# A two-layer cross-attention network on one Trainium2 core: three positions moved in the self-attention's hand-written order

## The reference

```
x1 = x  + MHA(LN(x), LN(ctx))          # layer 0 cross-attention, 16 heads of 32
x2 = x1 + MLP(LN(x1))                  # layer 0, hidden width 2048
x3 = x2 + MHA(LN(x2), LN(x2))          # layer 1 self-attention  <- the change is in here
x4 = x3 + MHA(LN(x3), ctx)             # layer 1 cross-attention
x5 = x4 + MLP(LN(x4))                  # layer 1, hidden width 2048
```

## Time and profile before

| | |
|---|---|
| median of three runs | 3421.28 us |
| the profiled execution | 3420.01 us |
| its span, first to last instruction | 3418.2 us |
| mean granted TensorE clock over the span | 0.962 of 2.4 GHz |
| the self-attention stage | from about 1280 to 2257 us of the span |
| idle of TensorE in it for the low part of the attention output (L105) | 26.7 us in 8 waits, the longest 10.3 |

### The profile page before, as it was taken

How to read it: one execution, slowest core, us unless ns; L and a number is a source line. 1 busy time by engine, 2 the same in 40 slices (tenths; PEclk the granted TensorE clock), 3 DMA queues, 4 the chain that set the end, 5 groups by cost and what they waited for, 6 DMA issues and landing times. The chain is left out here.

```text
span 3418.2 us, 41927 instructions
## 1 busy us (share of the span) xinstructions
PE 3165.7 (93%) x14480; PEld 2513.7 (74%) x14480; DVE 1801.5 (53%) x2848; ACT 1573.0 (46%) x2980; POOL 1322.0 (39%) x1355
## 2 busy tenths in 40 slices
PE   6599997999999977999999999849999799999999
PEld 5378776888888855777777777537878588888887
DVE  4588863322322224777777777748887432222221
ACT  2366653322222214766676677626666332222222
POOL 0344441333333332666666666734554111111110
PEclk8799998999999987999999999979999899999999
DMA  4423213211111114443344334331321321111000
GB/s 139 120 58 84 86 53 120 77 50 50 50 44 50 38 48 120 110 119 100 105 123 121 107 105 109 93 105 52 90 81 56 111 81 37 38 37 38 29 30 29
DMA packets 215045, 264.33 MB, mean 77 GB/s; under 512 B 78459, under 2 KB 100579, under 8 KB 214835
## 3 DMA queue, kind: packets, MB, share of 16 engines
q1 hardware_dynamic: 214835, 261.66, 25.7%
HBM read 125.12 MB, written 60.42 MB: 54 GB/s over the span
## 5 line engine op out<-in xcount | busy, mean ns | idle before, releaser
L1101 DVE TENSOR_REDUCE L1sa_nmax<-L1sa_s 128x2 f32<-128x1024 f32 x256 | 310.6, 1213 | 159.9 <-PE L1sa_s L907 159.9
L1206 POOL TENSOR_TENSOR L1sa_El<-L1sa_E,L1sa_Eh 128x1024 fp32r<-128x1024 f32 x128 | 313.3, 2448 | 150.6 <-ACT L1sa_Eh L1000 142.7
L468 DVE TENSOR_TENSOR L1ff_gl<-L1ff_gf,L1ff_gh 128x512 fp32r<-128x512 f32 x128 | 94.9, 741 | 475.0 <-ACT L1ff_gh L428 475.0
L468 DVE TENSOR_TENSOR L0ff_gl<-L0ff_gf,L0ff_gh 128x512 fp32r<-128x512 f32 x128 | 97.1, 759 | 439.8 <-ACT L0ff_gh L428 439.8
L414 ACT ACTIVATE L1ff_gf<-L1ff_f,cols 128x512 f32<-128x512 f32 x128 | 88.3, 690 | 450.8 <-PE L1ff_f L94 450.8
L414 ACT ACTIVATE L0ff_gf<-L0ff_f,cols 128x512 f32<-128x512 f32 x128 | 88.3, 690 | 450.4 <-PE L0ff_f L94 450.4
L1009 ACT ACTIVATE L1sa_E<-L1sa_st 128x1024 f32<-128x1024 f32 x256 | 258.6, 1010 | 8.8 <-PE L1sa_st L919 8.7
L92 PE MATMUL L1ff_f<-L1ff_hTh,L1ff_Wh 128*128 128x512 f32 x512 | 203.3, 397 | 5.7 <-POOL L1ff_hTl L235 5.7
L92 PE MATMUL L0ff_f<-L0ff_hTh,L0ff_Wh 128*128 128x512 f32 x512 | 203.1, 397 | 5.7 <-POOL L0ff_hTl L235 5.7
L1000 ACT ACTIVATE L1sa_Eh<-L1sa_E 128x1024 fp32r<-128x1024 f32 x192 | 200.5, 1044 | 0.2
L94 PE MATMUL L1ff_f<-L1ff_hTl,L1ff_Wh 128*128 128x512 f32 x512 | 200.4, 391 | 0.0
(11 more groups left out here) (282 smaller groups left out, 8514.4 us busy)
## 6 DMA issues: line engine op xcount, KB each, us to landing
L1sa_OLN<-L1sa_osb SPq DMA_DIRECT2D x128, 192.0 KB, 2.6
L0ff_xs<-x SPq DMA_DIRECT2D x64, 256.0 KB, 2.9
L1sa_stack_q<-L1sa_parts_q SPq DMA_DIRECT2D x128, 128.0 KB, 2.6
L1sa_stack_k<-L1sa_parts_k SPq DMA_DIRECT2D x128, 128.0 KB, 2.6
L1ff_xs<-x SPq DMA_DIRECT2D x64, 256.0 KB, 3.3
L0ca_xs<-in_x SPq DMA_DIRECT2D x32, 256.0 KB, 3.0
L0ca_stage<-in_x SPq DMA_DIRECT2D x32, 256.0 KB, 2.8
x<-L0ca_stage SPq DMA_DIRECT2D x32, 256.0 KB, 2.0
```

Source lines behind the costliest of these rows:

```text
L468: nc.vector.tensor_tensor(gl[:, j % 2, :], gf[:, j % 2, :], f32(gh[:, j % 2, :]), ALU.subtract)\
L1101: nc.vector.reduce_max(nmax[:, h % 2, 2 * (n % 2):2 * (n % 2) + 2], s_bank[:, :, :], AX.X, negate=True)\
L1206: nc.gpsimd.tensor_tensor(El[:, n % 2, :], E[:, n % 3, :], f32(Eh[:, n % 2, :]), ALU.subtract)\
```

## The change

Three positions in the written order change, and two DMA positions with them; no instruction is added or removed, and no buffer changes.

- T1, the transposition of the second tile of h, moves from half 24 to half 26 of the block, on TensorE, and with it the two instructions that take its result: ACT's and DVE's from s = 12 to s = 13.
- On SP the load of tile 3 of the next block's h moves from s = 13 to s = 14, and the load of tile 1 of the block after that from s = 16 to s = 17.
- `o_hi` on ACT and `o_lo` on DVE move: for group 0 of a block from n = 8g + 16 to 8g + 17 (s = 17), for the groups 1, 2 and 3 from n = 8g + 12 to 8g + 11 (s = 19, s = 27, and s = 3 of the next block).

```diff
-SA_T_HALVES = (22, 24, 28, 30)
+SA_T_HALVES = (22, 26, 28, 30)
...
-                    if s in (12, 13) and b + 1 < B:
-                        load(b + 1, 2 + (12, 13).index(s))
-                    if s in (15, 16) and b + 2 < B:
-                        load(b + 2, (15, 16).index(s))
+                    if s in (12, 14) and b + 1 < B:
+                        load(b + 1, 2 + (s - 12) // 2)
+                    if s in (15, 17) and b + 2 < B:
+                        load(b + 2, (s - 15) // 2)
...
-                        if n == 8 * g + (16 if g % G == 0 else 12):
+                        if n == 8 * g + (17 if g % G == 0 else 11):
                             o_hi(g)
...
-                        if n == 8 * g + (16 if g % G == 0 else 12):
+                        if n == 8 * g + (17 if g % G == 0 else 11):
                             o_lo(g)
```

## The result

The changed kernel takes 3467.38 us (median of four runs, 3462.45 to 3471.11) where the one before takes 3423.08 us beside it: the ratio is 1.0129, with a 95% interval of 1.0111 to 1.0147. It is slower, as forecast, but by 44 us and not by 22: the time lies 5 us above the upper end of the range. The profiled execution took 3465.93 us, its span is 3464.1 us, and the mean granted clock is 0.959.

A forecast was written before the change was run, and what follows sets the result against it. TensorE, busy 93% of the span, was taken as the bound. O0 - 23.2, ACT + 11.5, T3 + 27.8, clock + 13 and recovery - 5.5 gave + 23.6 on 3420.01 us: forecast 3443, range 3420 to 3462 us.

The forecast's parts named there:

- is done before O0 is due: At s = 3, the moved `o_lo` stands behind the earlier scores' maximum and finishes before TensorE's O0 needs it.
- its 0.7 us: At s = 19, group 0's `o_lo` delays DVE's `o_inverse` by 0.7 us; ACT's 0.5 us waits become 1.1.
- O0: TensorE at s = 4: seven waits for `o_lo` go, gaining 17.7 us plus 5.5 of clock, 23.2 us.
- Group 0: Its `o_hi` and `o_lo` moving from s = 16 to s = 17 was costed at nothing.
- ACT's term: ACT's `o_hi` meets POOL's `onorm`, so `exp` is late: 0.5 us at 23 places, 11.5 us lost, between 0 and 25.
- What is late next: nothing, rather the reverse.: At s = 16 to 18, SP, POOL and DVE catch up while TensorE waits: 5.5 us back, between 0 and 7.
- T3: Tile 3's transposition waits for its late load: 3.76 us in six blocks, 5.2 in block 0, 27.8 us, plus 13 of clock.
- The three waits without a fall: Three of seven O0 waits in the kernel before cost no clock, so the clock loss needn't come every time.
- The sum: Against 3420.01 us: - 23.2 + 11.5 + 27.8 + 13 - 5.5 = + 23.6, so 3443.6 us.
- The third rival: ACT's late `exp` costs 1.1 us at 23 places, clock 2.5 us in seven blocks: + 47, 3467 us; chance 0.07.
- The range's lower end: The forecast's own range, from its clock and ACT bounds, was 3425 to 3462 us.

The follow-up runs named there:

- experiment 8: Kernel before, with TensorE waiting for group 3's `o_lo` only at O0's fourth quarter and at the first for group 2's: 3397.03 us, ratio 0.9930.
- experiment 5: Kernel before, with tile 3's load at s = 14 and group 0's `o_hi` and `o_lo` at s = 17, other groups unmoved: 3469.77 us, ratio 1.0143.
- experiment 6: Kernel of experiment 5, with POOL's `e_lo` in step 17 cut to 16 of its 1024 columns: 3449.56 us, ratio 1.0086.
- experiment 2: Kernel before, with only `o_hi` and `o_lo` moved as in the change: 3425.90 us, ratio 1.0011.
- experiment 3: Changed kernel, with tile 3's load first in s = 14, ahead of `line_up` and the eight copies: 3424.23 us, ratio 1.0007.

## Why the prediction was wrong

**The step that failed** is the cost of the moved `o_lo`. I took its duration from its old places (0.68 to 0.98 us) to its new ones: "is done before O0 is due", "its 0.7 us" at s = 19, and group 0, which "I cost at nothing". All its old places are in even steps, where DVE has its own `e_lo`, and POOL has nothing beside it or shorter instructions (but for one place in the last block, where it meets the end of an `e_lo`); all its new ones are in odd steps, where POOL has its `e_lo`, and there `o_lo` ends half a us after POOL's instruction. I looked at who waits for whom, never at who runs beside whom. The trace of before had the sign: the earlier trace rows show group 3's `o_lo` at 0.98 us where groups 0 and 2 take 0.68, and I passed over it. What stands beside it there is POOL's rounding of the probabilities:

```profile
1578.52 1.04 POOL L1199 CAST L1sa_Eh<-L1sa_E 128x1024 fp32r<-128x1024 f32 x1
```

It ends at 1579.56, and `o_lo` at 1579.12 + 0.98 = 1580.10, 0.54 us later: about the distance that the 28 long ones have in the changed kernel.

**O0: - 23.2 forecast, - 14.8 measured.** The wait of 2.3 us became one of 0.9, because `o_lo` takes 2.58 us; step 4 takes 4.6 us in the seven blocks where 3.39 was forecast. The clock no longer falls behind any of the seven (granted clock 1.00 in the 4 us behind each), so that part of the term came. The sum was right in size for a wait that really goes (experiment 8: - 23.5). That POOL's `e_lo` makes the 0.9 us is worked out from the trace; no experiment shortened POOL's instruction at step 3.

**Group 0: nothing forecast, some 18 to 22 us measured**, and not in its own step but two steps on, as a wait for the row maximum. This is the largest error. Experiments 5 and 6 show it: moving group 0 in the presence of T3's wait costs 22 us, and shortening POOL's instruction beside it gives 20 back. The prediction did see that group 0's `o_lo` pushes `o_inverse` back, as a bound of ACT's term, but at 0.7 us and with ACT as the one that waits for it.

**"What is late next: nothing, rather the reverse."** The recovery was real: steps 17 and 18 gave back 7.2 us, where 5.5 was forecast. But that recovery brings POOL on time, and so its `e_lo` lies on `o_lo`. Without T3's wait (experiments 2 and 3) POOL is late, and group 0's `o_lo` gets ahead of `e_lo`. So the term that I booked as a gain set up the loss. Nothing in the sum could hold this, since it is in neither part alone.

**T3: 27.8 + 13 forecast, 38.8 measured** in steps 15 and 16. The wait is 3.6 to 3.8 us in blocks 1 to 6, against 3.76 forecast; block 0 has 4.5 where 5.2 was forecast, and its T2 waits 1.4 us instead of 0.6. Beyond the waits steps 15 and 16 lost another 1.6 to 2.5 us in each of the seven blocks, 13.0 together, which I put down to the clock: it fell during or behind all seven waits, to a mean of 0.50 to 0.74 in the 3 us behind. The three waits without a fall, on which the prediction's doubt rested, were waits of 2.3 us. This step, the decisive one for the sign, was right in place and size.

**ACT's lateness: + 11.5 forecast;** L919's waits for ACT rose by 11.4 us, in 20 more places instead of 23.

**The sum:** O0 fell short by 8.4 us, and steps 19 and 20 have 22.1 us where ACT's 4 was forecast: 26.5 us, against a miss of 22.3 on the profiled execution; the rest are small differences the other way. The third rival has the right total, 3467 us, by luck: ACT's part came out at its forecast, and it had no collision on DVE in it. The range's lower end was mis-added as well: by the prediction's own bounds it is 3420.0 - 23.2 + 27.8 - 5.5 = 3419, not 3425, which doesn't bear on the miss.

## What to carry to other kernels

Moving an instruction on its engine's order also moves it beside other instructions of other engines: before its duration is carried over, look at what POOL does in the new place, above all if the moved one is on DVE and reads two SBUF tiles. When a change adds a wait, follow who catches up during it, since an engine that is suddenly on time can collide where it was late before. And a wait can often be removed at the reader, by waiting only at the part that reads the late data: here that brought the time to 0.9930 of the kernel before (0.9916 to 0.9945), where `o_hi` and `o_lo` a step earlier gave nothing (1.0011) and `o_lo` ahead of the maximum gave less (0.9953).

## What the runs showed of the hardware

DVE's subtraction of two SBUF tiles of 128x512 takes 0.68 us alone; issued beside a POOL subtraction of 2.4 us it took 2.28 to 2.59 us in 28 of 32 cases of the changed kernel, and in all 28 it ended some 0.55 us after POOL's. Beside a POOL cast of 1.04 us it took 0.98. The other way round POOL's instruction takes longer: in the changed kernel's last block `o_lo` is issued 0.04 us ahead of `e_lo`, keeps its 0.68 us, and `e_lo` takes 2.88 instead of 2.4:

```profile
2238.28 0.68 DVE L105 TENSOR_TENSOR L1sa_oTl<-L1sa_onorm,L1sa_oTh 128x512 fp32r<-128x512 f32 x1
...
2238.32 2.88 POOL L1206 TENSOR_TENSOR L1sa_El<-L1sa_E,L1sa_Eh 128x1024 fp32r<-128x1024 f32 x1
```

The profile counts the standstill as busy time, not as a wait: only the duration gives it away. The same operation with one operand in PSUM isn't held up in the two cases that lie wholly inside a POOL subtraction (0.68 and 0.69 us); here is one, DVE first and then POOL (changed kernel):

```profile
1383.87 0.68 DVE L1139 TENSOR_TENSOR L1sa_hTl<-L1sa_pj,L1sa_hTh 128x512 fp32r<-128x512 f32 x1
...
1382.47 2.38 POOL L1206 TENSOR_TENSOR L1sa_El<-L1sa_E,L1sa_Eh 128x1024 fp32r<-128x1024 f32 x1
```

Nor are the row maxima, which read PSUM alone: 72 of them lie wholly inside a POOL subtraction, at 1.20 to 1.23 us. The Trainium skill states this in "SBUF — State Buffer", section "Who interferes with whom": a DVE instruction with two inputs in SBUF contends with a GpSimd instruction that reads SBUF. Its section "Summary: rules for kernel authors" adds that the second one to issue stands fully still until the first is done. The trace agrees: POOL's `e_lo` kept its 2.37 to 2.41 us in the meetings of steps 3 and 17 shown above and `o_lo`, issued later, took the whole delay; where `o_lo` came first, `e_lo` took 2.84 and 2.88. I had not weighed that page in the prediction; with it, the 2.4 us of POOL's `e_lo` at s = 3 and s = 17 would have been a term of the sum.
